# Self attention: four of a batch's twelve key transfers are issued by GpSimd, eight stay on the sync queue

## The reference

```
x = x + self_attention(layernorm(x))          # 16 heads of 8; mask: blocks of 64 tokens, and 8 global tokens
x = x + cross_attention(layernorm(x), ctx)    # 64 context rows a batch, then a small MLP
x = x + moe(layernorm(x))                     # 16 experts, 2 a token, and a shared expert
```

## Time and profile before

| | |
|---|---|
| time, median of 3 runs | 567.05 us (566.04 to 572.32) |
| time of the profiled execution | 568.54 us |
| span of the profiled execution | 566.7 us |
| mean granted TensorE clock | 0.961 of full speed |
| PE busy | 469.9 us (83%) |
| DVE busy | 409.6 us (72%) |
| POOL busy | 298.4 us (53%) |
| ACT busy | 296.8 us (52%) |

### The profile page before, as it was taken

How to read it: one execution, slowest core, us unless ns; L and a number is a source line. 1 busy time by engine, 2 the same in 40 slices (tenths; PEclk the granted TensorE clock), 3 DMA queues, 4 the chain that set the end, 5 groups by cost and what they waited for, 6 DMA issues and landing times. The chain is left out here.

```text
span 566.7 us, 17496 instructions
## 1 busy us (share of the span) xinstructions
PE 469.9 (83%) x6139; PEld 348.1 (61%) x6139; DVE 409.6 (72%) x1247; ACT 296.8 (52%) x757; POOL 298.4 (53%) x588
## 2 busy tenths in 40 slices
PE   1977888888888888888999999999767999999810
PEld 1755666666666666545676676666544888888610
DVE  7566999999888888876889898987572434434337
ACT  2573665555556656524656656564424444444237
POOL 5543454444444334201358888777771577777720
PEclk9997999999999999969999999999989999999975
DMA  6626343455655655326233333332124334333158
GB/s 189 112 51 139 55 71 63 67 132 111 110 108 110 108 107 114 81 52 150 54 83 90 95 87 97 96 85 67 34 97 132 106 110 116 110 109 98 53 178 286
DMA packets 96006, 58.30 MB, mean 103 GB/s; under 512 B 24560, under 2 KB 92224, under 8 KB 95920
## 3 DMA queue, kind: packets, MB, share of 16 engines
q1 hardware_dynamic: 74448, 39.93, 30.2%
q10 hardware_dynamic: 16896, 7.34, 6.7%
q0 software_dynamic: 4576, 9.91, 5.1%
HBM read 20.76 MB, written 17.50 MB: 68 GB/s over the span
## 5 line engine op out<-in xcount | busy, mean ns | idle before, releaser
L507 POOL TENSOR_SCALAR veps<-mv 128x2 f32<-128x2 f32 x48 | 11.2, 232 | 144.9 <-issue 101.2
L1292 ACT ACTIVATE probs<-ps 128x512 f32<-128x512 f32 x128 | 73.3, 603 | 12.1 <-PE ps L1672 9.8
L613 POOL DMA_INDIRECT expert_in<-xn,sloti x64 | 65.5, 1023 | 17.6 <-issue 17.6
L1147 DVE TENSOR_TENSOR eh<-ps,sg 128x256 f32<-128x256 f32 x40 | 17.0, 425 | 59.8 <-ACT sg L1496 58.9
L772 DVE TENSOR_REDUCE nmax<-ps 128x8 f32<-128x512 f32 x64 | 42.5, 686 | 18.9 <-PE ps L1607 18.8
L666 POOL DMA_INDIRECT expert_out<-ey,xt x40 | 38.3, 957 | 27.0 <-DVE ey L1154 16.7
L772 DVE TENSOR_REDUCE mparts<-ps 128x8 bf16<-128x512 f32 x64 | 43.3, 687 | 6.7 <-PE ps L1662 6.3
L1607 PE MATMUL ps<-kbd,qs 96*64 96x128 bf16 x512 | 38.0, 293 | 4.5 <-DMA qs<-part 3.6
L2026 PE MATMUL ps<-wgu,turned 128*128 x160 | 41.3, 380 | 0.0
L1490 ACT COPY turned<-ps 128x512 f32<-128x512 f32 (+1 forms) x43 | 23.8, 554 | 28.5 <-PE ps L2019 23.2
L509 POOL TENSOR_TENSOR rstd<-veps,minus_half 128x2 f32<-128x2 f32 x48 | 35.8, 745 | 4.0
(11 more groups left out here) (248 smaller groups left out, 1360.2 us busy)
## 6 DMA issues: line engine op xcount, KB each, us to landing
kbd<-part SPq DMA_DIRECT2D x192, 32.0 KB
qs<-part ACTq DMA_DIRECT2D x93, 64.0 KB
xt<-expert_in SPq DMA_DIRECT2D x64, 72.0 KB
qs<-part SPq DMA_DIRECT2D x51, 64.0 KB
ck_scr<-wgu SPq DMA_DIRECT2D x6, 512.0 KB
ckbd<-ck_scr SPq DMA_DIRECT2D x16, 192.0 KB
kbd<-part SPq DMA_DIRECT2D x48, 64.0 KB
wgu<-in_L_ffn_gate_up_w SPq DMA_DIRECT2D x4, 512.0 KB, 4.0
```

The source lines that it names most:

```text
L613: pool.indirect_dma_start(xs, bass.IndirectOffsetOnAxis(sloti[b % 3][:, n:n + 1], 0), xn3[b % 3][:, n // TOPK, n % TOPK, :], None).then_in ...
L1292: a_.activation(probs[:, 2 * i:2 * i + 2, :], P2[i % 2][:, :].rearrange("p (j q) -> p j q", j=2), ACT.Exp, scale=SCALE).then_inc(s("probs" ...
```

## The change

GpSimd gets the four transfers of the combinations i = 4 (part 1) and i = 2 (part 2) of every batch, through a new function `keys_regrouped`; SP keeps the other eight, and no other instruction changes its place in its engine's order. GpSimd calls the function for batch b + 1 behind `self_global_heads(b + 1)`, ahead of the memset and of `rstd_of`; for batch 0 it stands in the preparation, behind `rstd_of(s_, 1)`. The function waits for part 1, issues two transfers, waits for part 2, and issues two more. The four count up a semaphore of their own, `lent`, and whoever waited for `got` now waits for `lent` too: SP at the end of its batch, PE ahead of both halves of the scores of blocks 0 and 1, ACT ahead of part 0, GpSimd ahead of the global keys. To stay within the number of semaphores, the global keys count up `kgqg` with the global heads, three a batch instead of two, and the waits on it are renumbered.

```diff
-        GOT = {True: 16 * 3 * NP, False: 16 * NP}
+        LENT = 4
+        GOT = {True: 16 * (3 * NP - LENT), False: 16 * NP}
+        def by_pool(b, i):
+            return i in (2, 4)
+        def headed(b):
+            return 3 * b + 2
...
@@ SP, regroup_self
-                        if K_PART[i] == k:
+                        if K_PART[i] == k and not by_pool(b, i):
                             for a in range(2):
                                 sp.dma_start(kbd[p][16 * i + 8 * a:16 * i + 8 * a + 8, :, a, :, :].rearrange("r j k n -> r j (k n)"),
                                              part[64 * a:64 * a + 64, k, S:2 * S]).then_inc(s_("got"), 16)
...
-                wait_apart(sp, (s_("got"), GOT[True] * b + GOT[True]))
+                wait_apart(sp, (s_("got"), GOT[True] * b + GOT[True]), (s_("lent"), 16 * LENT * (b + 1)))
...
@@ GpSimd
             def self_global_keys(b, p):
                 pool.wait_ge(s_("got"), GOT[True] * b + GOT[True])
+                pool.wait_ge(s_("lent"), 16 * LENT * (b + 1))
...
-                last.then_inc(s_("kbg"), 1)
+                last.then_inc(s_("kgqg"), 1)
+
+            def keys_regrouped(b, p):
+                at_least(pool, s_("gk_ps"), b - 1)
+                for i in (4, 2):
+                    pool.wait_ge(s_("part"), 3 * b + K_PART[i] + 1)
+                    for a in range(2):
+                        pool.dma_start(kbd[p][16 * i + 8 * a:16 * i + 8 * a + 8, :, a, :, :].rearrange("r j k n -> r j (k n)"),
+                                       part[64 * a:64 * a + 64, K_PART[i], S:2 * S]).then_inc(s_("lent"), 16)
...
-                pool.wait_ge(s_("kgqg"), 2 * b + 4)
+                pool.wait_ge(s_("kgqg"), headed(b + 1))
...
                     self_global_heads(b + 1, 1 - p)
+                    keys_regrouped(b + 1, 1 - p)
...
             rstd_of(s_, 1)
+            keys_regrouped(0, 0)
             order(2, cwq)
             self_global_heads(0, 0)
...
@@ ACT, self_first_part (and once at the start of the cross attention)
-                at_least(act, s_("kgqg"), 2 * b - 2)
+                at_least(act, s_("kgqg"), headed(b - 2))
...
                 at_least(act, s_("got"), GOT[True] * b)
+                at_least(act, s_("lent"), 16 * LENT * b)
...
@@ PE
             def self_scores(b, p, u, half):
                 if u == 0:
                     pe.wait_ge(s_("got"), GOT[True] * b + GOT[True])
+                    pe.wait_ge(s_("lent"), 16 * LENT * (b + 1))
...
             def self_global_scores(b, p):
-                pe.wait_ge(s_("kgqg"), 2 * b + 2)
+                pe.wait_ge(s_("kgqg"), headed(b))
...
             def global_keys(b, p):
                 pe.wait_ge(s_("probs"), 4 * b + 3)
-                pe.wait_ge(s_("kbg"), b + 1)
+                pe.wait_ge(s_("kgqg"), headed(b) + 1)
```

More of the change, by code:

```diff
@@ L1305, in cross_first_part @@
                     act.wait_ge(s_("got"), GOT[True] * B)
+                    act.wait_ge(s_("lent"), 16 * LENT * B)
                 at_least(act, c_("got"), GOT[False] * (b - 1))
```

## The result

The changed kernel took 574.27 us (median of 9 runs, 569.53 to 576.54), the one before 568.47 beside it: a ratio of 1.0096, 95% interval 1.0056 to 1.0136. It is 1.0% slower where 0.5% faster was forecast. The profiled execution took 573.95 us, its span is 572.1, against 568.54 and 566.7.

What follows compares the result with a forecast made beforehand. PE was taken to bound the self attention, with short waits for DVE and ACT. Ordinary batches 1.2 us plus batch 1's 1.7 take 2.9 us off 568.54, giving 565.6, a median of 564.1; range 560.8 to 571.

Steps and rivals of the forecast that it cites:

- GpSimd's price: Each key transfer issued by GpSimd costs 1.26 us (0.96 plus a 0.30 gap), taken from its indirect transfers of 128 rows.
- The lower bound, SP's price: Low end for GpSimd's issue: 0.61 us, SP's median for the same transfer; with it batch 1 gives 4.1 us.
- GpSimd becomes the bound: Rival, chance 0.15: from 1.54 us an issue the 1 / sqrt is late in fourteen batches; at 1.73 a median of 576.
- the copies: Rival, chance 0.05: DVE's two shift-row copies wait for GpSimd's issues, 1.9 us a batch, 29 us, a median near 592.
- Landing: GpSimd's transfers land 2.3 us after their start; in an ordinary batch the last at 161.9, 1.5 us ahead of PE.
- neither queue late any more, the 1.2 us come back in full: Ordinary batches: keys from both queues arrive in time, so PE's waits for transfers, worth 1.2 us, all go.
- Nothing: Rival, chance 0.10: GpSimd's share lands about as late as SP's did, or transfers, not issues, set the landing; about 567.
- I count no difference: What SP issues behind the four starts 2.7 us earlier, now beside GpSimd's last transfers instead of SP's: no effect.
- they land at about 22.9: nothing: Preparation: GpSimd's four of batch 0 land at about 22.9, ahead of the scores at 26.31, so no effect.
- Batch 1: Earlier keys let PE's scores begin 2.4 us earlier, but PE then waits for GpSimd's global heads: gain 1.7 us.
- Sum: 1.2 + 1.7 = 2.9 us off 568.54, giving 565.6; expected median 564.1, 0.5% faster.
- my slower rival: The slower-side rival, chance 0.15: GpSimd's issues delay its 1 / sqrt from 1.54 us each; at 1.73 a median of 576.

Runs made afterwards that it cites:

- x_waits: The changed kernel, but in batch 0 SP issues the 768 KB load of x only after all that batch's keys have landed: 569.96 us, 1.0024 against the kernel before.
- only0: The kernel before, but GpSimd issues its four key transfers in batch 0 alone, SP all twelve from batch 1 on: 570.82 us, 1.006.
- only1: The kernel before, but GpSimd issues its four key transfers in batch 1 alone: 565.74 us, 0.9964.
- from1: The changed kernel, but batch 0 keeps all twelve key transfers on SP: 567.37 us, 0.9994 against the kernel before.
- sp_small: The kernel before, SP issuing all twelve, but from batch 1 on the four carry an eighth of their bytes: 566.45 us, 0.9967.
- after_pos: The changed kernel plus already satisfied waits on GpSimd, moving its first indirect transfer of the cross attention 40 instructions further: 570.08 us, 1.0039 against the kernel before.
- loads_wait_pos: The changed kernel with SP's later loads behind each batch's keys, plus already satisfied waits lengthening GpSimd's program: 567.05 us, 0.9995 against the kernel before.
- loads_wait: The changed kernel, but in every batch SP's later loads wait until that batch's keys have landed: 569.16 us, 1.0041 against the kernel before.
- before_pos: The kernel before plus already satisfied waits on GpSimd, placing its first indirect transfer as far into the program as in the changed kernel: 574.21 us, 1.012.

## Why the prediction was wrong, step by step

- **GpSimd's price** was mis-sized: 0.56 us at the median, 2.34 to 2.53 for four with their gaps, where I took 1.26 each from an indirect transfer. The lower bound, SP's price, was the near one. This term and the rivals "GpSimd becomes the bound" and "the copies" fall with it: 3.18 us of idling were left where I reckoned 1.1 (0.5 with the memset of 0.6, which stands behind the issues in this batch and which I left out), and L806 beside the issues took 0.42.
- **Landing** was the first step that failed. I let GpSimd's transfers land 2.3 us after their start, a figure of indirect transfers in the expert stage; here they took 4.1 (median, x_waits) to 5.8 (only0's batch 0), and only in batch 1 3.0 (only1). So "neither queue late any more, the 1.2 us come back in full" is wrong: from1 gains nothing, and what batch 1 gains in it is lost again behind it. sp_small shows why: with as many issues on SP but fewer bytes the waits go. In an ordinary batch the movement sets when keys come, and two queues brought them no earlier than one. The Trainium skill's rule that I weighed and set aside ("DMA: Bandwidth & Descriptors", "Issuing engines are not separate DMA queues") was right of these batches, and of the rivals the one called "Nothing" came true there.
- **"I count no difference"** for what SP issues behind was the step that cost the sign. In batch 0 the load of x moved 2.65 us forward, beside GpSimd's four, and "they land at about 22.9: nothing" became 3 us of standing. (That they would lie in GpSimd's own idling was right: they took 3.94 us of it.) only0 puts the price at 0.6%, x_waits takes it away.
- **Batch 1**: I took 1.7 us, with 4.1 at the low price. Its wait fell from 3.97 to 1.22, and from its scores to the next it took 13.04 us instead of 14.00, now at a full clock: 3.7 in the trace; by only1 it is worth 2.0 us in time. Right in mechanism, as SP's fifteen issues were what was late. That 1.7 is near 2.0 is luck: it rests on the price of 1.26 and on PE waiting for GpSimd's heads at its global scores, and in the changed kernel's trace it doesn't wait for them there. What the added waits cost by themselves no run shows.
- **The stand** in the cross attention is in none of my steps: 64 transfers with their waits lengthen GpSimd's program, and an instruction some 70 us behind the last of them stood 2.57 us. after_pos against the changed kernel, 1.0039 against 1.0096, gives it 0.57%; loads_wait_pos against loads_wait 0.46%. The intervals overlap in both pairs; that two pairs agree, and the stand goes in both traces, carries it.
- **Sum**: +0.60 (only0) - 0.36 (only1) + 0.46 to 0.57 (the stand) is 0.70 to 0.81%, inside the measured 0.56 to 1.36. The fourteen ordinary batches are not in it: from1 against only1 puts them at +0.30, not clear of noise, and with them it is 1.00 to 1.11%. I had no case for code that merely grows, and my slower rival had the wrong mechanism.

What stays open: how much the ordinary batches lose, and why. From the scores of batch 2 to those of batch 15 the eight traces in which GpSimd issues whole transfers there take 169.0 (from1) to 172.5 us (x_waits; 172.0 in the changed kernel). The five in which SP issues all of them take 167.3 to 169.2, with before_pos, which its 1 / sqrt lengthens, left out. So they seem to lose, and part of the 3.2 us between the second and the first landmark is this; one execution each doesn't give the size. Nor is it shown that the later loads cause it. A wait ahead of them gained 0.15, 0.19 and 0.38% in from1, only1 and the kernel before, of which only the last is clear of noise, and its 2.2 us are more than the 1.2 us of waits that I had found there. Between x_waits and loads_wait it gained nothing (1.0024 and 1.0041, intervals overlapping).

## What to carry to other kernels

Ask of a late transfer whether its issue or its movement is late: shrink its bytes at the same number of issues, and see whether the wait goes. When issues leave a queue, look at what stands behind them there: a large load that starts earlier takes the DMA engines from the very transfers that were to be sped up, and one wait ahead of it repaired that in batch 0 here. And when a change adds instructions, compare stands by "issue" in stages that it doesn't touch, and shift the program by some idle instructions before you judge it.

## What the runs showed of the hardware

- The place of an instruction in GpSimd's program is worth 2.4 to 2.6 us of standing. That it is the loading of code is inferred: in the 3.5 us around the stand of the changed kernel the instruction queue moved two packets, shown below by the table of queues. This is a weak hint, as it moved one in the 3.5 us ahead of the same transfer in the kernel before, which didn't stand. The Trainium skill, "Runtime: NRT & Kernel Launch", "Instruction fetch mechanics", says that the sequencer fetches its program in blocks through a DMA queue, at a cost mostly hidden; here, in four kernels, it was not hidden, if it was that.

```profile
q14 instruction: 2, 0.02, 1.9%
```

- A plain transfer of 64 rows of 512 bytes costs GpSimd 0.56 us to issue, less than SP's 0.61, and lands 3.0 us (batch 1, only1) to 4.2 us (loads_wait) later at the median.
- GpSimd's 1 / sqrt takes 0.72 us when it begins 0.03 us ahead of a two-input operation of DVE, and 1.81 when it begins 0.01 ahead.
